# Two slots in place of three, and spare products in TensorE's loop, in a matrix product that streams 268 MB

## The reference

```python
# x, u: (8192, 64) fp32;  adj: (8192, 8192) fp32, mostly zeros but stored and read dense
keep = (u >= 0.1).astype(x.dtype)
x_drop = x * keep / (1.0 - 0.1)
y = x + jnp.matmul(adj, x_drop)
out = (y - mean(y)) / sqrt(var(y) + 1e-5)      # over the 64 columns of each row
```

## Time and profile before

| | us |
|---|---|
| median of 3 runs | 642.44 (642.42 to 642.57) |
| the profiled execution | 642.77 |
| its span, first to last instruction | 640.9 |
| its mean granted TensorE clock | 0.918 |
| TensorE busy | 516.3 (81% of the span) |
| VectorE, ScalarE, GpSimd busy | 52.1, 10.8, 18.0 |
| moved by DMA | 274.83 MB, mean 429 GB/s |

### The profile page before, as it was taken

One profiled execution on the slowest core, in us unless ns is written; L12 is line 12 of the kernel. 1 busy time (PEld: TensorE's weight loads), 2 busy tenths in 40 slices (PEclk: granted clock), 3 DMA queues, 4 the chain that ended last, 5 costly groups with the idle time before them and its releaser, 6 DMA issues.

```text
span 640.9 us, 5635 instructions
## 1 busy us (share of the span) xinstructions
PE 516.3 (81%) x2308; PEld 176.5 (28%) x2308; DVE 52.1 (8%) x231; ACT 10.8 (2%) x18; POOL 18.0 (3%) x27
## 2 busy tenths in 40 slices
PE   0397797887977886897879869787887879879996
PEld 0122222232322322232222223222222223223325
DVE  5100101000010100001010010100001010010102
ACT  0000000000000000000000000000000000000000
POOL 0000000000000000000000000000000000000000
PEclk9997997988989899897989898898998889898999
DMA  9999999999999999999999999999999999999998
GB/s 383 424 448 432 429 430 443 413 440 426 439 428 450 421 441 437 433 427 443 413 440 429 430 432 449 424 441 435 431 431 439 414 443 428 429 429 431 429 424 347
DMA packets 9794, 274.83 MB, mean 429 GB/s; under 512 B 1216, under 2 KB 1472, under 8 KB 2496
## 3 DMA queue, kind: packets, MB, share of 16 engines
q1 hardware_dynamic: 9504, 274.63, 99.5%
q10 hardware_dynamic: 288, 0.16, 0.1%
HBM read 272.66 MB, written 2.13 MB: 429 GB/s over the span
## 4 chain that ended last, share of the span: by engine, by line
DMA 70%; PE 27%; issue 1%; SPq 0%; DVE 0%; POOL 0%; POOLq 0%; ACT 0%; DVEq 0%
DMA raw<-adj_dram 70%; PE acc L170 27%; SPq L131 0%; PE turned L190 0%; POOL rstd L275 0%; DVE stats L245 0%; POOLq L46 0%; ACT sums L216 0%; DVE rows L241 0%; SPq L135 0%; SPq L134 0%; DVE moments L250 0%; POOLq L280 0%; DVE final_normed L268 0%; DVE var_eps L253 0%
## 5 line engine op out<-in xcount | busy, mean ns | idle before, releaser
L170 PE MATMUL acc<-raw,dropped 128*64 128x504 f32 x2048 | 490.5, 639 | 91.4 <-POOLq L280 90.0
L170 PEld LDWEIGHTS acc<-raw,dropped 128*64 128x64 f32 x2048 | 153.3, 148 | 416.7 <-issue 294.0
L241 DVE TENSOR_TENSOR rows<-turned,x_sb 126x256 f32<-126x256 f32 x16 | 6.8, 424 | 544.4 <-PE turned L190 544.4
L275 POOL TENSOR_TENSOR rstd<-var_eps,minus_half 126x4 f32<-126x4 f32 x16 | 16.2, 1011 | 613.2 <-DMA raw<-adj_dram 328.3
L190 PE MATMUL turned<-join,sums 128*126 128x64 f32 x128 | 17.5, 279 | 10.9 <-ACT sums L216 10.9
L190 PEld LDWEIGHTS turned<-join,sums 128*126 128x126 f32 x128 | 15.3, 189 | 24.8 <-ACT sums L216 24.8
L216 ACT COPY sums<-acc 128x504 f32<-128x504 f32 x16 | 9.2, 578 | 616.1 <-PE acc L170 616.1
L256 DVE TENSOR_SCALAR normed<-rows,moments,rstd 126x64 f32 x64 | 15.7, 309 | 26.7 <-POOL rstd L275 26.7
L180 PE MATMUL final_turned<-x_sb,eye 128*128 128x64 f32 x2 | 0.7, 448 | 17.9 <-DVE dropped L235 17.9
L245 DVE BATCH_NORM_STATS2 stats<-rows 126x6 f32<-126x64 f32 x64 | 9.7, 214 | 0.5
L170 PE MATMUL final_acc<-raw,dropped 128*64 128x128 f32 x124 | 7.1, 275 | 0.0
(11 more groups left out here) (17 smaller groups left out, 3.5 us busy)
## 6 DMA issues: line engine op xcount, KB each, us to landing
raw<-adj_dram SPq DMA_DIRECT2D x30, 5544.0 KB, 26.8
raw<-adj_dram SPq DMA_DIRECT2D x14, 5040.0 KB, 29.2
raw<-adj_dram SPq DMA_DIRECT2D x2, 3024.0 KB, 21.3
raw<-adj_dram SPq DMA_DIRECT2D x2, 2520.0 KB, 26.9
raw<-adj_dram SPq DMA_DIRECT2D x2, 2016.0 KB, 21.3
raw<-adj_dram SPq DMA_DIRECT2D x2, 1512.0 KB, 24.6
x_sb<-x_dram SPq DMA_DIRECT2D x1, 2080.0 KB, 12.1
dropped<-u_dram SPq DMA_DIRECT2D x1, 2048.0 KB, 7.6
```

The costliest lines, as they stand in the source:

```text
L170: last = nc.tensor.matmul(sum_bank[t * D:(t + 1) * D, 0:width], dropped[:, t * PAIRS + q, :], raw[:, s, start:start + width], start=(q == ...
L241: nc.vector.tensor_tensor(rows[:, :, :], turned[0:ROWS, 0:GROUPS, :], x_sb[0:ROWS, bass.ds(b * GROUPS, GROUPS), :], ALU.add).then_inc(turn ...
L275: nc.gpsimd.tensor_tensor(rstd[:, :], var_eps[:, :], minus_half[0:ROWS, :], ALU.pow).then_inc(rstd_ready, 1)
```

## The change

The slots become two of 16 pairs each (pairs 0 to 16 and 16 to 32), so that an ordinary block has two loads of 8.3 MB in place of three, and `raw` has room for 32 pairs where it had room for 33. Slot 0 of block 0 is now loaded in its three parts (6, 5, 5 pairs), slot 1 of block 14 in two pieces (JOINED: parts 3 and 4, parts 5 to 7), block 15 in eight parts, as before but for the third, fourth and fifth, which are (11, 16), (16, 22), (22, 26) where (11, 17), (17, 22), (22, 26) were.

TensorE gets products that nobody reads (`keep_busy`): weights `dropped[:, 0:2, :]` (128 x 128), 504 columns of `dropped` streaming, result in a bank of its own, `spare`. In each of the 14 blocks of its loop there are three ahead of the block's first wait, five between slot 0 and slot 1, and one between the last product and the wait for the copy. The last two blocks are written out behind the loop; block 14 has the three at its top alone, block 15 none. GpSimd's waits are counted anew for the new parts.

```diff
--- before.py
+++ after.py
@@ -19,14 +19,20 @@
-SLOT_PAIRS = [(0, 11), (11, 22), (22, 32)]
+SLOT_PAIRS = [(0, 16), (16, 32)]
 SLOTS = len(SLOT_PAIRS)
 SLOT = max(q1 - q0 for q0, q1 in SLOT_PAIRS) * PAIR
-PARTS = [(0, 0, 6), (0, 6, 11), (1, 11, 17), (1, 17, 22), (2, 22, 26), (2, 26, 29), (2, 29, 31), (2, 31, 32)]
+PARTS = [(0, 0, 6), (0, 6, 11), (0, 11, 16), (1, 16, 22), (1, 22, 26), (1, 26, 29), (1, 29, 31), (1, 31, 32)]
+JOINED = [(3, 5), (5, 8)]
 IN_SLOT = [sum(part[0] == s for part in PARTS) for s in range(SLOTS)]
 FINAL = [(0, 8), (8, 16), (16, 22), (22, 26), (26, 29), (29, 31), (31, 32)]
+IDLE_TOP, IDLE_SLOT, IDLE_COPY = 3, 5, 1
@@ -79,6 +85,7 @@
         turned = psum("turned", [P, 512 // D, D])
         final_acc = psum("final_acc", [P, 512])
         final_turned = psum("final_turned", [P, 512])
+        spare = psum("spare", [P, 512])
         x_loaded = semaphore("x_loaded")
         u_loaded = semaphore("u_loaded")
@@ -120,11 +127,11 @@
         @block.sync
         def _(sp):
-            def load_part(b, n):
-                s, q0, q1 = PARTS[n]
+            def load_parts(b, n0, n1):
+                s, q0, q1 = PARTS[n0][0], PARTS[n0][1], PARTS[n1 - 1][2]
                 q_slot = SLOT_PAIRS[s][0]
                 sp.dma_start(raw[:, s, (q0 - q_slot) * PAIR:(q1 - q_slot) * PAIR],
-                             adj[b, :, q0 * PAIR:q1 * PAIR]).then_inc(part_loaded[n], DMA)
+                             adj[b, :, q0 * PAIR:q1 * PAIR]).then_inc(part_loaded[n0], DMA)
             def load_slot(b, s):
                 q0, q1 = SLOT_PAIRS[s]
@@ -133,23 +140,22 @@
             sp.dma_start(dropped[:, :, :], u_dram).then_inc(u_loaded, DMA)
             sp.dma_start(x_sb[:, :, :], x).then_inc(x_loaded, DMA)
-            for s in range(SLOTS):
-                load_slot(0, s)
+            for n in range(IN_SLOT[0]):
+                load_parts(0, n, n + 1)
+            load_slot(0, 1)
             with sp.Fori(1, BLOCKS - 2) as b:
                 for s in range(SLOTS):
                     sp.wait_ge(multiplied, (b - 1) * SLOTS + s + 1)
                     load_slot(b, s)
-            for s in range(SLOTS - 1):
-                sp.wait_ge(multiplied, (BLOCKS - 3) * SLOTS + s + 1)
-                load_slot(BLOCKS - 2, s)
-            sp.wait_ge(multiplied, (BLOCKS - 2) * SLOTS)
-            for n, (s, q0, q1) in enumerate(PARTS):
-                if s == SLOTS - 1:
-                    load_part(BLOCKS - 2, n)
+            sp.wait_ge(multiplied, (BLOCKS - 3) * SLOTS + 1)
+            load_slot(BLOCKS - 2, 0)
+            sp.wait_ge(multiplied, (BLOCKS - 3) * SLOTS + 2)
+            for n0, n1 in JOINED:
+                load_parts(BLOCKS - 2, n0, n1)
             for n, (s, q0, q1) in enumerate(PARTS):
                 if q0 == SLOT_PAIRS[s][0]:
                     sp.wait_ge(multiplied, (BLOCKS - 2) * SLOTS + s + 1)
-                load_part(BLOCKS - 1, n)
+                load_parts(BLOCKS - 1, n, n + 1)
             sp.wait_ge(multiplied, (BLOCKS - 1) * SLOTS + 1)
             pair = TILES * P
@@ -163,6 +169,12 @@
         @block.tensor
         def _(pe):
+            def keep_busy(times):
+                for _ in range(times):
+                    nc.tensor.matmul(spare[:, 0:WIDTH], dropped[:, 0:TILES, :],
+                                     dropped[:, :, :].rearrange("p c d -> p (c d)")[:, 0:WIDTH],
+                                     start=True, stop=True)
             def multiply(sum_bank, width, s, q_slot, q0, q1, pairs):
                 for q in range(q0, q1):
                     for t in range(TILES):
@@ -172,24 +184,33 @@
                                                 start=(q == 0), stop=(q == pairs - 1))
                 return last
-            pe.wait_ge(x_dropped, 1)
-            pe.wait_ge(x_loaded, DMA)
-            pe.wait_ge(eye_ready, 1)
-            pe.wait_ge(join_ready, 1)
-            nc.tensor.matmul(final_turned[:, 0:D], eye[:, :], x_sb[:, CHUNKS, :], start=True, stop=False)
-            with pe.Fori(0, BLOCKS) as b:
+            def multiply_block(b, idle_top, idle_slot, idle_copy):
+                keep_busy(idle_top)
                 for n, (s, q0, q1) in enumerate(PARTS):
                     pe.wait_ge(landed, b * len(PARTS) + n + 1)
                     last = multiply(acc, WIDTH, s, SLOT_PAIRS[s][0], q0, q1, PAIRS)
                     if q1 == SLOT_PAIRS[s][1]:
                         last.then_inc(multiplied, 1)
+                        if s == 0:
+                            keep_busy(idle_slot)
+                keep_busy(idle_copy)
                 pe.wait_ge(sums_ready, b + 1)
                 for i in range(GROUPS):
                     last = nc.tensor.matmul(turned[0:ROWS, i, :], sums[:, i * ROWS:(i + 1) * ROWS], join[:, :],
                                             start=True, stop=True)
                 last.then_inc(block_turned, 1)
+            pe.wait_ge(x_dropped, 1)
+            pe.wait_ge(x_loaded, DMA)
+            pe.wait_ge(eye_ready, 1)
+            pe.wait_ge(join_ready, 1)
+            nc.tensor.matmul(final_turned[:, 0:D], eye[:, :], x_sb[:, CHUNKS, :], start=True, stop=False)
+            with pe.Fori(0, BLOCKS - 2) as b:
+                multiply_block(b, IDLE_TOP, IDLE_SLOT, IDLE_COPY)
+            multiply_block(BLOCKS - 2, IDLE_TOP, 0, 0)
+            multiply_block(BLOCKS - 1, 0, 0, 0)
             q_last = PAIRS - 1
@@ -276,12 +297,13 @@
                                         ALU.pow).then_inc(rstd_ready, 1)
             def pass_slot(b, s):
-                pool.wait_ge(raw_loaded[s], b * DMA + DMA)
+                pool.wait_ge(raw_loaded[s], b * DMA if s == 0 else b * DMA + DMA)
                 pool.sem_inc(landed, IN_SLOT[s])
-            def pass_part(n, loads):
-                pool.wait_ge(part_loaded[n], loads * DMA)
-                pool.sem_inc(landed, 1)
+            def pass_parts(n0, n1, loads):
+                pool.wait_ge(part_loaded[n0], loads * DMA)
+                pool.sem_inc(landed, n1 - n0)
             nc.gpsimd.memset(minus_half[:, :], -0.5).then_inc(minus_half_ready, 1)
             nc.gpsimd.memset(eye[:, :], 0.0).then_inc(squares_zeroed, 1)
@@ -296,19 +318,17 @@
                                     base=-D, pattern=[[-1, D]], channel_multiplier=1).then_inc(join_ready, 1)
             pool.wait_ge(minus_half_ready, 1)
-            pass_slot(0, 0)
+            for n in range(IN_SLOT[0]):
+                pass_parts(n, n + 1, 1)
             with pool.Fori(0, BLOCKS - 2) as b:
-                for s in range(1, SLOTS):
-                    pass_slot(b, s)
+                pass_slot(b, 1)
                 pass_slot(b + 1, 0)
                 rsqrt(b)
-            for s in range(1, SLOTS - 1):
-                pass_slot(BLOCKS - 2, s)
+            for n0, n1 in JOINED:
+                pass_parts(n0, n1, 1)
             for n, (s, q0, q1) in enumerate(PARTS):
-                if s == SLOTS - 1:
-                    pass_part(n, 1)
-            for n, (s, q0, q1) in enumerate(PARTS):
-                pass_part(n, 2 if s == SLOTS - 1 else 1)
+                pass_parts(n, n + 1, 2 if s == 0 or any(n == n0 for n0, n1 in JOINED) else 1)
                 if n == 1:
                     rsqrt(BLOCKS - 2)
             rsqrt(BLOCKS - 1)
```

More of the change, by code:

```diff
@@ L173, in multiply @@
                 return last
+            def multiply_block(b, idle_top, idle_slot, idle_copy):
+                keep_busy(idle_top)
+                for n, (s, q0, q1) in enumerate(PARTS):
+                    pe.wait_ge(landed, b * len(PARTS) + n + 1)
+                    last = multiply(acc, WIDTH, s, SLOT_PAIRS[s][0], q0, q1, PAIRS)
+                    if q1 == SLOT_PAIRS[s][1]:
+                        last.then_inc(multiplied, 1)
+                        if s == 0:
+                            keep_busy(idle_slot)
+                keep_busy(idle_copy)
+                pe.wait_ge(sums_ready, b + 1)
+                for i in range(GROUPS):
+                    last = nc.tensor.matmul(turned[0:ROWS, i, :], sums[:, i * ROWS:(i + 1) * ROWS], join[:, :],
+                                            start=True, stop=True)
+                last.then_inc(block_turned, 1)
             pe.wait_ge(x_dropped, 1)
```

## The result

| | before | changed |
|---|---|---|
| median | 642.55 us (642.27 to 642.79, 9 runs) | 644.30 us (643.48 to 645.06, 9 runs) |
| profiled execution, its span | 642.77, 640.9 | 644.22, 642.4 |
| mean granted clock | 0.918 | 0.991 |

The ratio is 1.0028, 95% interval 1.0018 to 1.0039: slower by 1.8 us. The prediction held no change likeliest (643.1 us); the measured time lies inside its range. The runs of the changed kernel also scatter over 1.6 us, those of before over 0.5.

The account below looks back on a forecast made before the run. DMA transfers were taken to bound the kernel. To 642.77 us it added +0.7 (clock hole at pair 16), 0 for queue depth, spares and code, -0.05 for parts: 643.4 profiled, 643.1 median; range 642.3 to 645.0.

Parts of the forecast that it names:

- Transfers set the time: Steady loop: DMA transfers, not TensorE's clock, set the time; 1.192 us a pair, 38.13 us a block.
- Nothing per transfer: Adjacency loads: cost goes by bytes, not by count, so fewer, larger slots change nothing; taken as 0.
- The spares: TensorE's loop: spare products end before the next landing, idle 0.6 to 1.0 us a slot, clock stays up; worth 0.
- rival 4: End of each slot: two slots don't cover the reload; 0.6 us per such slot, up to 17 us; chance 0.06.
- Queue depth: Slot reloads: the other slot's 19.07 us cover products, issue and start with 2.3 us left; no DMA gap, cost 0.
- Block 0: Start-up: TensorE starts slow and leaves block 1's slot 0 at 87.4, queue covered to 89.6; cost 0, bounded by 1.3.
- Code: Blocks 14 and 15: two or so more instruction fetches, each holding one DMA engine back 1.28 us; taken as 0.
- Rival 3: Block 15 landings: an added code fetch hits the engine that is already last; +1.5 to +3 us, 645; chance 0.08.
- The hole in block 15: Before pair 16: TensorE waits 2.9 us, the next run is likely slow by 1.6 us; +0.7 us at the end.
- rival 1: Block 15: the clock holds through the 2.9 us wait; +0.0, 642.4 us; chance 0.14.
- rival 2: Block 15: the clock falls for longer, 2.7 us lost, +1.8 at the end, 644.2 us; chance 0.15.
- The tail: Last row store: issued at 639.8 but takes 1.4 us on emptied engines, so only 0.7 of 1.6 us reach the end.

Follow-up runs that it names:

- slot 0 whole: The changed kernel with slot 0 of block 0 loaded whole in place of in three parts; 643.93 us median, ratio 1.0020.
- slot 1 in pieces: The changed kernel with slot 1 of block 0 loaded in two pieces (10 and 6 pairs) in place of one; 644.22 us, ratio 1.0032.

## Why the prediction was right or wrong

**Transfers set the time, 1.192 us a pair whatever the slot.** Right to 0.1%: 38.10 us a block for 38.13. "Nothing per transfer" was read off slots of 11 and 10 pairs, and it holds there; from three slots to two it is 0.03 us a block, from four to three 0.13. The proportion 11/10 couldn't show that.

**The spares.** Their price and fit were right (4.49 us for five, idle of 0.85 to 0.89). "Worth: 0, because it was hidden" was wrong as a statement on two slots: without them the time is 654.6. Both halves were there, the clock hidden with three slots and rival 4 for two; the run without spares is rival 4 with the clock left to fall. As a term against the kernel before, the 0 stands.

**Queue depth.** The step that failed: "19.07 - 13.8 - 0.15 - 2.8 leaves 2.3 us. No gap in the DMA. Cost 0." I bounded the way from issue to data by the first load, 2.8 us, on engines that had nothing else to do, and took it for an upper bound. In the changed kernel a reload issued 3.0 us before the other slot had landed (68.48, 71.46) came 1.09 us late, one issued 5.0 us before (86.61, 91.60) 0.41 us late. Landing less issue less 19.05 us of bytes is 4.1 and 5.4 us for these two, where I had 2.8. There is no sharp limit: in the other kernels with two slots and spares, reloads issued 3.6 us ahead came 0.7 to 1.2 us late, one issued 3.3 us ahead 0.15; with slot 0 whole one 4.9 us ahead (66.59, 71.46) cost nothing, and neither did the loop's, 5.0 ahead (144.12, 149.16). The trace's DMA packets say where the 1.09 us went. The 16 engines took up their new shares 1.15 to 3.04 us after the issue at 68.48, with up to five of them idle at one time. The last of the old shares ended at 71.02, the last of the new ones began at 71.52, 0.50 us later, and its first packet took 2.96 us in place of 2.38, 0.58 us more: together the 1.09. So half of it is the way to the data, 3.0 us on the slowest engine, and half is packets that run slower while a new load starts, a term that I did not have at all. Behind the loop's issue at 144.12 no engine stood idle and no packet was slow, but the first engine took up its new share 2.67 us after the issue, so little of the 2.3 us of slack is left.

**Block 0.** "Just enough ... Cost 0, bounded by 1.3": the late reloads cost 1.5 us; as the first code fetch cost 0.5 us and not 1.3, 0.8 us of it were left against the kernel before. The times of the stretch were right (slot 1 lands at 51.87 for 51.5, its run ends at 68.3 for 68). The allowance was wrong, by the step above, and I checked one reload only, that of slot 0 (87.4 against 89.6). The one before it, of slot 1, was the later one, and by my own numbers it had 70.6 - 68 = 2.6 us for the 2.95 that I took a reload to need.

**Code.** The number of fetches (four) and their size were right, that they fall on other engines too. That this makes them free was an argument from three slots, where it is true (642.76). The Trainium skill ("Runtime: NRT & Kernel Launch", Instruction fetch mechanics) calls the crossing of a 16 KiB boundary mostly hidden; it speaks of the engine that fetches, and for the loads that share the DMA engine the landings here differ from it. With two slots the late reloads of blocks 1 and 2 leave the early engines idle (up to five of 16 at one time behind the issue at 68.48, up to three behind that at 86.61). After them the lead is 0.37 us, where it was 1.27 before; it stays so through the loop. The late reloads alone aren't the reason: with slot 0 whole, where no landing of blocks 1 and 2 after the first was late, the lead is 0.30 us all the same. What takes it there isn't shown; packets of up to 3.23 us for 2.38 stand behind its reload at 66.59. Then the two added fetches make the landings late, by 0.6 to 1.35 us together. Rival 3 had this effect, at +1.3 a fetch, with the wrong condition: no two fetches need share an engine, and a single one cost between nothing and 1.2 us. The first fetch, in turn, cost 0.5 us here and 1.3 before.

**The hole in block 15.** Right in place and size (2.73 us) and in what it does when the clock falls: 1.70 us lost in the run, last store issued at 639.79 as reckoned (639.8), 0.7 us more span, all measured with slot 0 whole. In the changed kernel's own profile the clock held (rival 1's case). Of the five profiles of two slots with that hole unfilled, it fell in three (slot 0 whole, and both kernels without spares, 15.44 us each) and held in two (changed; slot 1 in pieces). I had given its fall 67% (the forecast and rival 2).

**The tail.** That part of a late TensorE is absorbed while the queues drain held in that case. It doesn't hold for late loads: in the changed kernel the last store is issued at 639.78, the same, but the engines are 1.6 us behind too, it takes 2.3 us, and the span is 642.4.

So the sum was short by late loads: +0.7 was expected from the clock, and the profiled execution has 0 from the clock and +1.6 from the loads. The likeliest case was not the one that came; it is a mixture of rivals 3 and 4, to which I gave 14% together. Of the 35% for slower by over 0.2%, 15 came from rival 2, which no run of two slots showed. That rival 2's 644.2 us is the measured time to 0.1 us is luck, and so is that the time lies in the range: I had left rival 4, half of the cause, out of it.

**What stays open.** How the nine runs of the changed kernel divide between clock and fetches: a run that isn't profiled tells neither. Why packets are slower while a new load starts. Why a fetch costs 0 in one execution and 1.2 us in another. Whether without any fetch during the loads three slots would gain their 1.3 us; it wasn't tried. No version ran faster than the kernel before.

## What to carry to other kernels

Count a buffer's depth by the whole way from the last read of a slot to the first bytes of the next load on every engine, with the queues in use, not by an idle first load, and check every reload of the start-up, not one; here 19.05 us of cover for 13.9 us of work was the edge. A semaphore of 16 engines waits for the slowest: look at how far the others are ahead before you call a disturbance of one engine free, since a deep queue hides such things and a thin one lets them through. When an engine is kept warm because a queue became thin, ask first whether the old queue needed it.

## What the runs showed of the hardware that I had not expected

A reload issued 3 to 5 us before the slot ahead of it landed still came 0.4 to 1.1 us late, where the first 2 MB, on idle queues, needed no more than 2.8 us beside their bytes. The engines took up its packets 1.15 to 3.04 us after the issue, and a packet of 64512 bytes took up to 3.07 us there for 2.38 in the steady loop. The same bytes in 2, 3 and 4 transfers a block took 38.10, 38.13 and 38.26 us. The Trainium skill ("DMA: Bandwidth & Descriptors", Anatomy of one DMA; written of GpSimd's path) has some 2.0 us fixed for each DMA. Of that 0.03 and 0.13 us are seen here for one more a block, where the next is queued already. An idle of 2.7 us with products on both sides left the clock at its upper level in two executions (13.74 us) and not in three others (15.44).
